# Moving the base inverse's steps on GpSimd's list, the block stores on SyncE's queue and one exponential on ScalarE in a fused two-layer kernel

## What is computed

```python
def step(S, inp):                      # one token, state S is (heads, 128, 128)
    qt, kt, vt, gt, bt = inp
    S = S * jnp.exp(gt)[:, None, None]
    kv = jnp.einsum('hk,hkv->hv', kt, S)
    delta = (vt - kv) * bt[:, None]
    S = S + kt[:, :, None] * delta[:, None, :]
    o = jnp.einsum('hk,hkv->hv', qt, S)
    return (S, o)
```

## Time and profile before

| | |
|---|---|
| median of 3 runs | 2868.48 us (2863.65 to 2868.64) |
| the profiled execution, its own time | 2868.26 us |
| its span | 2866.6 us |
| TensorE (PE) busy | 2700.8 us, 94% of the span |
| VectorE (DVE) busy | 2196.3 us, 77% |
| ScalarE (ACT) busy | 1823.8 us, 64% |
| GpSimd (POOL) busy | 1534.7 us, 54% |
| DMA queue of SyncE | 19.1% of 16 engines' span |
| mean granted clock of TensorE | 0.98 |

### The profile page before, as it was taken

The page is one execution under the profiler, slowest core; times in us unless marked ns, Lnnn a source line. Parts: engine busy times, 40 slices in busy tenths (PEclk is TensorE's granted clock), DMA queues, the critical chain, the costliest instruction groups (busy, mean ns, idle before and its releaser), DMA issues. The chain is left out here.

```text
span 2866.6 us, 75659 instructions
## 1 busy us (share of the span) xinstructions
PE 2700.8 (94%) x24303; PEld 1879.6 (66%) x24303; DVE 2196.3 (77%) x4677; ACT 1823.8 (64%) x6310; POOL 1534.7 (54%) x3737
## 2 busy tenths in 40 slices
PE   5999679999999999999999999999999999869998
PEld 4556357776777776776777667767766776645555
DVE  3443468888888888888888888888888888637775
ACT  3322467777777777777777777777777776323332
POOL 1000277666777666776766677776667776210000
PEclk9999889999999999999999999999999999969999
DMA  4000121222222222223222222222222222010000
GB/s 93 0 1 0 27 53 37 56 44 54 43 49 40 51 50 48 51 42 52 37 53 46 55 41 50 41 48 46 54 46 47 53 37 46 18 44 1 8 8 15
DMA packets 485567, 113.69 MB, mean 40 GB/s; under 512 B 423296, under 2 KB 484336, under 8 KB 485168
## 3 DMA queue, kind: packets, MB, share of 16 engines
q1 hardware_dynamic: 485168, 108.76, 19.1%
HBM read 80.63 MB, written 28.06 MB: 38 GB/s over the span
## 5 line engine op out<-in xcount | busy, mean ns | idle before, releaser
L548 POOL TENSOR_TENSOR Tb<-Tb,btmp 64x14 f32<-64x14 f32 (+6 forms) x896 | 369.1, 412 | 71.9 <-issue 1.7
L544 POOL TENSOR_TENSOR btmp<-Bk,Tb 64x14 f32<-64x14 f32 (+6 forms) x896 | 353.6, 395 | 60.6 <-POOL Tb L536 0.2
L1231 DVE SCALAR_TENSOR_TENSOR S<-S,gs,bank 128x128 f32<-128x128 f32 x1024 | 287.2, 342 | 46.8 <-PE bank L787 28.2
L933 ACT ACTIVATE oq<-bank,gs 128x128 f32<-128x128 f32 x512 | 160.2, 364 | 241.2 <-PE bank L624 241.2
L1127 DVE SCALAR_TENSOR_TENSOR R<-bank,gs,xn 128x128 f32<-128x128 f32 x512 | 155.8, 346 | 183.2 <-PE bank L613 183.1
L1262 DVE SCALAR_TENSOR_TENSOR conv<-raw,ckq,conv 128x512 f32<-128x512 f32 x384 | 284.7, 755 | 14.5 <-ACT conv L1016 7.4
L1262 DVE SCALAR_TENSOR_TENSOR conv<-raw,cv,conv 128x512 f32<-128x512 f32 x384 | 282.3, 749 | 8.6 <-ACT conv L1016 1.5
L759 PE MATMUL bank<-wz_h,xnT 128*128 128x256 f32 x1024 | 263.5, 380 | 0.0
L743 PE MATMUL bank<-xnT,wkq 128*128 128x512 f32 x512 | 241.2, 614 | 10.6 <-POOL mkX L429 10.6
L832 PE MATMUL bank<-wout_h,gT 128*128 128x256 f32 x1024 | 246.4, 384 | 0.1
L1014 ACT ACTIVATE raw<-bank 128x512 f32<-128x512 f32 x256 | 154.0, 601 | 144.9 <-PE bank L743 144.9
(11 more groups left out here) (354 smaller groups left out, 6704.2 us busy)
## 6 DMA issues: line engine op xcount, KB each, us to landing
rowb<-decay_rows SPq DMA_DIRECT2D x256, 64.0 KB, 4.0
blk_n<-N SPq DMA_DIRECT2D x256, 64.0 KB, 2.2
Tp<-blk_t SPq DMA_DIRECT2D x128, 128.0 KB, 2.9
Wp<-blk_w SPq DMA_DIRECT2D x128, 128.0 KB, 3.0
wkq<-in_L_attn_W_qkvz_dram SPq DMA_DIRECT2D x32, 128.0 KB, 2.2
wv<-in_L_attn_W_qkvz_dram SPq DMA_DIRECT2D x16, 256.0 KB, 2.6
Bk<-blk_n SPq DMA_DIRECT2D x64, 64.0 KB, 2.6
blk_t<-Tb SPq DMA_DIRECT2D x64, 64.0 KB, 2.6
```

What stands on the lines that cost most here:

```text
L544: pool.tensor_tensor(tmp, Bk[:, j, j + 1:].unsqueeze(2).broadcast_to([64, 15 - j, j]), Tb[:, j, 0:j].unsqueeze(1).broadcast_to([64, 15 - j ...
L548: pool.tensor_tensor(Tb[:, j + 1:, 0:j], Tb[:, j + 1:, 0:j], tmp, ALU.subtract).then_inc(row_rdy, 1)
L933: i = act.activation(oq[t.c % 2][:, u, :], pQS[:, v], ACT.Copy, scale=gs[t.c][:, GAM, u:u + 1])
L1231: i = dve.scalar_tensor_tensor(out=S[:, 2 * b + v, :], in0=S[:, 2 * b + v, :], scalar=gs[t.c][:, kind, 2 * h + v:2 * h + v + 1], in1=pKU[b ...
```

## The change

Three orders are rewritten; no instruction is added or dropped.

```diff
@@ -387,7 +387,7 @@
 
                 def base_load(s):
 
-                    t = s.back(S_F + 1)
+                    t = s.back(S_F)
                     if not t.live or t.c % 2 == 0:
                         return
                     sent, free = held(sp, t.at(32, 32)), held(sp, t.pairs())
@@ -397,14 +397,14 @@
                     sp.dma_start(Bk[:], blocks(nd)).then_inc(blk_in, 16)
 
                 def body(s):
-                    base_load(s)
                     decays(s)
+                    base_out(s)
+                    value_weights(s)
                     key_weights(s)
-                    value_weights(s)
                     gate_weights(s)
                     out_weights(s)
-                    base_out(s)
                     dump(s)
+                    base_load(s)
                 pipeline(sp, body)
                 sp.wait_ge(t_in, 32 * PAIRS)
                 sp.wait_ge(w_in, 32 * PAIRS)
@@ -553,7 +553,7 @@
                     if not t.live or t.c % 2 == 0:
                         return
                     base_start(t)
-                    for j in range(1, 5):
+                    for j in range(1, 4):
                         base_row(t, j)
 
                 def base_middle(s):
@@ -561,7 +561,7 @@
                     t = s.back(S_F + 1)
                     if not t.live or t.c % 2 == 0:
                         return
-                    for j in range(5, 11):
+                    for j in range(4, 11):
                         base_row(t, j)
 
                 def base_rest(s):
@@ -589,11 +589,11 @@
                 def body(s):
                     step_gates(s)
                     halo(s)
+                    base_rest(s)
+                    base_first(s)
                     derive(s)
                     scaled(s)
                     causal(s)
-                    base_rest(s)
-                    base_first(s)
                     out_scale(s)
                     base_middle(s)
                     norm_scale(s)
@@ -1059,7 +1059,6 @@
                     kdec(s)
                     clamp(s)
                     silu(s)
-                    expo(s)
                     evac(s, 0)
                     squares(s)
                     from_state(s, 1)
@@ -1067,6 +1066,7 @@
                     normed(s)
                     vscale(s)
                     gtev(s)
+                    expo(s)
                     ztanh(s)
                     low_rank_ev(s)
                     norm_ev(s)
```

## The result

| | before | changed |
|---|---|---|
| median | 2868.24 us (2863.65 to 2868.64, 4 runs) | 2891.22 us (2886.16 to 2891.42, 4 runs) |
| profiled execution, its span | 2866.6 us | 2889.7 us |

The ratio is 1.008, 95% interval 1.0062 to 1.0097: **slower by some 23 us.** The forecast was 2884, the range 2848 to 2906. The kernel before had one more run here, which moves its median from 2868.48 to 2868.24.

What follows compares the result with a forecast made beforehand. TensorE, busy 94% of the span, was taken as the bound, with 33 us of waits above a floor of 16.40 us a round. 2868.26 − 29 (opening rounds mainly) + 45 (closing rounds) = 2884 us, range 2848 to 2906.

Steps and rivals of the forecast that it cites:

- the loss: Closing rounds: GpSimd's late ETn delays TensorE 0.75 us in 59 rounds, plus 1 at loop restarts: +45 us.
- the gain: Waiting above the 16.40 us floor removed: 26 us in opening rounds, the rest in closing ones, −29 us in all.
- The chain of a closing round: GpSimd's rows ahead of derive, then VectorE's holds, make ETn ready at 8.87, holding strict, R and TensorE's solve.
- the slack of TensorE: Closing rounds, before solve: 0.15 us of R's 0.90 us delay absorbed, leaving TensorE held 0.75 us.
- The opening rounds: SyncE's new order and first rows ahead of derive make a late Bk harmless to out_scale: −26 us.
- opening rounds fall to the floor: Opening rounds return to 16.40 us, worth −26 us, except three that stand apart with 3.5 us.
- (1): Closing rounds: VectorE's hold on GpSimd misses ETn, rounds stay at 16.40, kernel 2839 us; chance 0.17.
- (2): Closing rounds: derive's second product passes between the holds, 0.5 us lost per round, 2869 us; chance 0.15 shared with (4).
- (3): Round's end: base_start also holds VectorE's convolution taps, adding 12 to 30 us, 2905 with the rest; chance 0.13.
- (4): Whole kernel: nothing comes of it, TensorE's 94% covers both sides, within 0.2% of 2868; chance 0.15 shared with (2).
- The signs: Profile: gatn wait gone, TensorE waits some 45 us for R, VectorE about 1.2 for ETn, GpSimd idles before L533, L514.
- `expo` and SyncE at nothing: ScalarE's expo behind gtev, a forced move, and SyncE's decays going 5 us later: both cost nothing.

Runs made afterwards that it cites:

- e_split4: Changed kernel with rows 1 to 4 in base_first and 5 to 10 in base_middle, one row less ahead of a closing round's ETn: 2865.05 us.
- e_mid3: Changed kernel with rows 4 to 6 moved out of base_middle to between causal and out_scale, SyncE as changed: 2850.55 us, ratio 0.9945.
- e_mid3_k: Changed kernel with rows 4 to 6 between causal and out_scale, and SyncE's key weights alone moved behind the store of N: 2837.1 us, ratio 0.9878.
- e_split2: Changed kernel with rows 1 and 2 in base_first and 3 to 10 in base_middle, one row more ahead of ETn: 2907.14 us, ratio 1.0144.

## Why the prediction was right

**Sign and size.** 2884 predicted, 2891 measured: two opposed terms of which the loss is the larger, as forecast. As a difference it is 16 against 23 us: the loss was put some 6 us too low, the gain some 4 too high, and 2.9 us outside the 119 rounds, which no term of the prediction covers, made up for a part of both. So the total is a little closer than its terms are.

**The chain of a closing round.** Row by row, in us from the round's start: `ETn` ready predicted 8.87, measured 8.82; `strict` 8.94 and 8.94 (739.30 − 730.36); `R` ended 9.88 and 9.88. VectorE's wait of 1.2 us was announced and is there. The held instruction was to be the product that starts behind `silu`'s start (1.18 in place of 0.20 us), and the power before it was to slip through, which it did (1.04 us as ever).

**What was mis-sized there** is the slack of TensorE, "I give it 0.15". It was 0.11: `solve` now starts 9.99 − 9.88 = 0.11 behind `R`, where it started 0.22 behind the earlier trace rows. So it comes 0.79 us later, and the round's end 0.83 (17.23 against 16.40). In the rounds in which the loop starts again I counted 0.15 more; they last 17.57, 0.33 more, and seven others last 17.47. Together: 59 × 0.83 = 49 and some 3 more, 51.7 measured, 45 predicted.

**The opening rounds.** −26 predicted, −21.9 measured. The step that was too optimistic is "opening rounds fall to the floor": 7.7 us stay where I had left 3.5. 4.4 of them lie in the first round of the stretch (20.82 us, 19.38 before), 1.7 in two rounds of 17.23, the rest in rounds of 16.6. The chain itself ran as worked out, a little later: `base_start` at 16.2 where I had 15.3 (`N` is stored at 10.1, not 9.5), `derive` at 2.0, `ETn` at 4.8, far ahead of 7.7.

**The rivals.** (1), the hold misses `ETn`: not so, L465 is held. (2), half: no, L465 is held whole. `e_split4` shows the time of that case, by another row: there both products pass, and the next product and `ETn` are held. (3), VectorE held by `base_start`: the mechanism is there and the price is not. Just ahead of the opening round the five taps took 4.35 us (3.77 before), and VectorE's wait for TensorE behind them fell from 0.89 to 0.31: that idle time took all of the 0.58. In other rounds `base_start` is held too, up to 1.39 us in place of 0.84, and the taps take 4.24. So both orders do cost VectorE nearly the same, as said, but 0.46 to 0.58 us and not the whole 0.84 of GpSimd's instruction. The timeline of VectorE, of the changed kernel:

```profile
743.63 4.35 DVE L1262 SCALAR_TENSOR_TENSOR conv<-raw,cv,conv 128x512 f32<-128x512 f32 x5
748.29 0.61 DVE L1127 SCALAR_TENSOR_TENSOR R<-bank,gs,xn 128x128 f32<-128x128 f32 x2 [0.31 <-PE bank L613]
```

(4), nothing: no.

**The signs.** VectorE's wait for `ETn` (1.2 us) and TensorE's ahead of `solve` (40.0 us in 60, where some 45 in 59 were named) are there, the wait for `gatn` is gone, and GpSimd's long idle times stand before L533 and L514. All as listed.

**`expo` and SyncE at nothing.** `expo` behind `gtev` costs nothing, as said, and had to move, as said: 166 us otherwise. What I did not see is how far the edits depend on each other: I put down −26 to SyncE and the first rows together, and the runs show +5 for the one alone and +69 (2960.22 − 2891.22) when only that one is missing. The gain hangs on a third edit that I did not name with it, `base_rest` ahead of `derive`: without it the kernel takes 3055 us. No run has SyncE's order and `base_rest` early with the first rows left behind `ETm`, so what the first rows give by themselves is not shown.

## What to carry to other kernels

An engine that is busy half the time can set the pace if its list puts a long block ahead of a small result that others wait for: follow the list from the last free moment to the moment at which the result is asked for, row by row, and add the holds by the other engine at the clock times at which they fall. Where two engines exclude each other, the same work costs nothing, 0.2 or 0.8 us a round (`e_mid3`, `e_split4`, the change), and each step between them is one row or a few; so try the cut at several places and not one. Split a long block over the idle times that its engine has, and reorder a queue only together with the producer that it waits for.

## What the runs showed of the hardware that I had not expected

A one-input `tensor_scalar` of VectorE over 128x1024 fp32 in SBUF held GpSimd for its whole 0.69 us, like the two-input form for its 1.22, while instructions of VectorE with one input in SBUF and one in PSUM did not hold it at all (`ETn` at 0.61 us, 62 times of 62 in `e_mid3_k`). And the hold costs whichever engine came second: a GpSimd product over four columns went from 0.20 to 1.18 us in the changed kernel. With one row fewer ahead of it (0.7 us) the loser is another instruction of GpSimd, `ETn`, 1.42 us in place of 0.61, and with one fewer still it is VectorE's `silu`, 1.22 to 1.74. A power over four columns, 1.04 us long, kept its length when it had begun ahead of the hold, and took 1.86 in `e_split2` when it began behind `silu`.
